# The first weight units of the experts split during the end of the attention, and the first gather's indices written by VectorE

## The chip, the cores and the metric

The kernel runs on one core of a Trainium2 chip, as one launch. A core has TensorE (PE in the profile; its weight loads are PEld), VectorE (DVE), ScalarE (ACT), GpSimd (POOL) and SyncE (SP), which only issues DMAs here. The metric is the device time of one execution in microseconds (us), as the median of several runs. Less is better.

## The reference, cut to what matters

The model is a gated cross-attention layer followed by a mixture of experts in which each expert picks its tokens:

```
x = x + tanh(g_xattn) * attention(layernorm(x), ctx, mask)        # B=8, S=224, D=512, context 750, 16 heads of 32
x = x + tanh(g_ffn)   * ffn(layernorm(x))
ffn(x):                                                            # E=8 experts, I=2048
    affinity = softmax(x @ gate_w.T), turned to (b, e, s)
    gating, idx = top_k(affinity, 56)                              # 56 rows for each batch and expert
    x_in = x[b, idx]                                               # gather
    h = silu(x_in @ w_gate.T) * (x_in @ w_up.T)
    out[b, idx] += gating * (h @ w_down.T)                         # scatter-add
```

All is float32. Expert 0 can start only once the top 56 rows of every batch are known, that is, after the attention and the second layer norm of the last batch.

## The kernel before, in words

There are three stages, each a block of its own. A block ends when every engine has come to its end, and the next one begins then.

**project_context** makes K and V of all batches. **attend** runs over the 8 batches: scores, softmax, values, output projection, residual (`x2`, in the tile `x_res`), second layer norm (`xn2`; the profile calls it `xn`), its rows stored to the DRAM tensor `xn_rows`, the logits of the gate and the affinities. Its functions `end()` (one for each engine) hold what is left for the last batch, and the change is there. On DVE (line 1165) the order is: the two `residual` operations (L1051), `moments` (L964, L967), `norm_2` (L975), the copy of the second half of the turned rows to `xT` (L1177), `logits` (L1061 to L1064), `affinity` (L1069 to L1074), and `rounds`: 7 rounds of MAX8, FIND_INDEX8 and MATCH_REPLACE8 (L1084 to L1086) for the top 56 and then `gate_all` and `row_all` (L1089, L1090). Between `moments` and `norm_2`, POOL turns the variance into 1/sqrt in two small operations (`root`, L780 and L782). POOL then stores the rows (`store_rows`, L810), writes the output rows' base (`x2_out`, two operations of line 795) and stores them (`store_out`, L806). ACT (line 941) copies `c_r` (L893), then the first half of the turned rows (`x2_columns`, L857), then takes the exponential of the logits (L897). PE turns the normed rows (`turn_last`, L1249) and computes the logits (L1262). SP, in its own `end()` (line 752), loads the last residual rows and then, once the last scores are made, the first 4 weight units (L756) into `w_raw`, which lies where `ks` was.

**experts** streams the weights as units of 128 x 1024 float32 (512 KB). There are 24 for each expert: 16 for gate and up, 8 for down. A unit has one of NRAW = 4 slots in each of `w_raw`, `w_hi` and `w_lo`. ACT copies it to fp32r (`ws_hi`, L1502), DVE writes the rest (`ws_lo = w_raw - ws_hi`, L1552), and PE makes three products for each pair of tiles (hi by hi, lo by hi, hi by lo: L1622 to L1624 for gate and up, L1639 to L1641 for down). Both splits run LEAD = 3 units ahead of PE; for the first three units of expert 0 they stand at the very start of this block, on ACT and on DVE. SP loads unit u as soon as the slot's `ws_lo` is written (`wlo_done`); for expert 0 that begins with unit 4.

The block begins with two small products on PE (L1668) that place the gates and the row numbers in `gu_ps[0]`. DVE takes `gate_t` (L1588) and `idx_t` (L1590) from there, POOL copies expert 0's four columns of `idx_t` to `gather_i` (L1469) and issues four indirect DMAs (L1472), each of 112 rows of 2 KB from `xn_rows` to `xg`. When all four have landed, PE turns them (L1608), ACT and DVE split them (`xs_hi` L1507, `xs_lo` L1557), and the first product of expert 0 can run. For the other experts the gather, the turning and the splitting run beside the products of the expert in front. `scatter(e)` copies four indices (L1477) and issues four indirect DMAs that add to the output (L1482).

In this stage the memory holds, from below: `h_hi`, `w_raw`, `w_hi`, `w_lo`, the gates and indices, `xg`, `xs_hi`, `xs_lo`, `silu`, `hid`, `h_lo`, `y_cols`, `y_sb`.

Of the kernel before, what the change touches and what calls it, by code (L numbers as in the profile page):

```python
# [7 lines left out]
F32R = mybir.dt.float32r  # L8
# [6 lines left out]
ds = bass.ds  # L15
# [27 lines left out]
LEAD = 3  # L43
WAYS = 32
# [25 lines left out]
F_XT, F_Q, F_USES = 0, 2, 4  # L70

# [46 lines left out]
def program(nc, ctxT, x, maskq, wk, wv, wq, wo, gatew, gx, gf, wstream, consts, rotations, out):  # L118
# [5 lines left out]
    with ExitStack() as top:  # L124
        def sem(name):
            return top.enter_context(nc.semaphore(name))
# [13 lines left out]
        w_in = [sem(f"w_in{j}") for j in range(NRAW)]  # L140

        with ExitStack() as mid:
# [8 lines left out]
            with ExitStack() as late:  # L151
                sb(late, "below", [P, IC * SLOTS - E_OVER * (KC // 2) * PAIR])
                w_raw = [sb(late, f"w_raw{j}", [P, UNIT]) for j in range(NRAW)]
# [5 lines left out]
                x_t=sb(mid, "x_t", [QP, QC, D]), xn=sb(mid, "xn", [QP, QC, D]), xT=sb(mid, "xT", [P, 2, 2 * S]),  # L159
                q_rot=sb(mid, "q_rot", [P, NG, S]), q_cos=sb(mid, "q_cos", [P, NG, S]),   # L160
                qs=sb(mid, "qs", [3 * WAYS, H, S], F32R), mq=sb(mid, "mq", [QP, QC, SK]),
# [12 lines left out]
                   cos, sin, gains, gate_all, row_all, wstream, w_raw, w_in)  # L174
        experts(nc, sem, sb, ps, w_raw, w_in, wstream, xn_rows, out_rows, cst, ident, gains, gate_all, row_all)
# [429 lines left out]
def attend(nc, sem, sb, ps, both, x, maskq, wo, gatew, kd, vd, xn_rows, out, cst, ident,  # L605
           cos, sin, gains, gate_all, row_all, wstream, w_raw, w_in):

    with ExitStack() as st:
# [77 lines left out]
        with nc.Block() as block:  # L686
            @block.sync
            def _(sp):
# [63 lines left out]
                def end():  # L752
                    load_res(B - 1)
                    hold(m_made, NS * B)
                    for u in range(NRAW):
                        sp.dma_start(w_raw[u][:], wstream[u]).then_inc(w_in[u], 16)  # L756
                    sp.wait_ge(x_in, 16 * (B + 1))
# [95 lines left out]
            def _(act):  # L853
# [87 lines left out]
                def end():  # L941
                    copy_parts(B - 1, NG - 1)
                    x2_columns(B - 1, 0)
                    logit_exp(B - 1)
# [4 lines left out]
            def _(dve):  # L949
# [143 lines left out]

                def start():
                    nc.vector.memset(flags_sb[:], 0.0).then_inc(rest_free, 1)
                    for h in range(MLEAD):
                        for qc in range(QC):
                            mask_scores(0, h, qc)
# [66 lines left out]
                def end():  # L1165
                    b = B - 1
                    normalise(b, NG - 2)
                    affinity(b - 1, (b - 1) % 2)
                    normalise(b, NG - 1)
                    for c in range(QC):  # L1170
                        residual(b, c, m_ps[c][0:QP, 0, :])
                    dve.wait_ge(rest_free, R_USES * b + R_Y + 3)
                    dve.nop(nofuse=True)
                    moments(b, 1, x2)
                    norm_2(b)
                    dve.wait_ge(rest_made, R_USES * b + R_XNT + 2)
                    nc.vector.tensor_copy(xT[:, 1], m_ps[1][:, 1, 0:2 * S]).then_inc(rest_free, 1)  # L1177
                    logits(b)
                    affinity(b, b % 2)
                    rounds()  # L1180
# [217 lines left out]
def experts(nc, sem, sb, ps, w_raw, w_in, wstream, xn_rows, out_rows, cst, ident, gains, gate_all, row_all):  # L1398

    with ExitStack() as st:  # L1400
        h_hi = sb(st, "h_hi", [P, IC, SLOTS], F32R)
        sb(st, "w_raw_place", [P, NRAW, UNIT])
        w_hi = [sb(st, f"ws_hi{j}", [P, UNIT], F32R) for j in range(NRAW)]
        w_lo = [sb(st, f"ws_lo{j}", [P, UNIT], F32R) for j in range(NRAW)]
# [3 lines left out]
        xg = sb(st, "xg", [RP, RG, D])  # L1408
        xs_hi, xs_lo = sb(st, "xs_hi", [P, DC, SLOTS], F32R), sb(st, "xs_lo", [P, DC, SLOTS], F32R)
        silu = [sb(st, f"silu{j}", [P, SLOTS]) for j in range(2)]  # L1410
        hid = [sb(st, f"hid{j}", [P, SLOTS]) for j in range(2)]
        h_lo = sb(st, "h_lo", [P, IC, SLOTS], F32R)
        y_cols = sb(st, "y_cols", [P, DC, SLOTS])
        y_sb = sb(st, "y_sb", [RP, RG, D])
# [5 lines left out]
        whi_done, wlo_done = sem("whi_done"), [sem(f"wlo_done{j}") for j in range(NRAW)]  # L1420
# [16 lines left out]
        with nc.Block() as block:  # L1437
            @block.sync
            def _(sp):
# [10 lines left out]

                for u in range(NRAW, NU):
                    load(0, u)
# [5 lines left out]
            def _(pool):  # L1458
# [5 lines left out]
                def gather(e):  # L1464


                    hold(x_turned, e)
                    hold(gathered, 16 * RG * e)
                    nc.gpsimd.tensor_copy(gather_i[:], idx_t[:, ds(e, 1), :].rearrange("p o g -> p (o g)")).then_inc(gidx_done, 1)  # L1469
                    hold(gidx_done, e + 1)  # L1470
                    for g in range(RG):
                        pool.indirect_dma_start(xg[:, g, :], None, xn_rows, bass.IndirectOffsetOnAxis(gather_i[:, g:g + 1], 0)).then_inc(gathered, 16)  # L1472
# [12 lines left out]
                pool.wait_ge(idx_ready, 1)  # L1485
# [10 lines left out]
            def _(act):  # L1496
# [39 lines left out]

                for u in range(LEAD):
                    split_w(0, u)
# [9 lines left out]
            def _(dve):  # L1548
# [38 lines left out]
                dve.wait_ge(turned, 1)  # L1587
                nc.vector.tensor_scalar(gate_t[:].rearrange("p e g -> p g e"), gu_ps[0][0:RP, 0:RG * E].rearrange("p (g e) -> p g e", g=RG),  # L1588
# [3 lines left out]
                for u in range(LEAD):  # L1592
                    split_w(0, u)
# [144 lines left out]
```

## Time and profile before

| | |
|---|---|
| three runs | 1839.09, 1839.38, 1833.33 us; median 1839.09 |
| the profiled execution | 1836.25 us |
| its span, first to last instruction | 1834.4 us |
| mean granted TensorE clock | 0.981 |
| PE busy | 1740.8 us (95%) |
| DVE, ACT, POOL busy | 1038.9, 839.2, 235.4 us |
| start of the experts' block | 841 us after the span's start |

The rows further down are of the one profiled execution; all their times count from the start of its span. A timeline row gives start, duration, engine, line, operation, written tile, read tiles and shapes, the number of instructions (x3: three, one behind the other, and the duration is then theirs together) and, in brackets, how long the engine had been idle before and what ended that. A row of a stretch gives its bounds and length, then for PE, PEld, DVE, ACT and POOL the busy time with the number of instructions, and then the granted TensorE clock (1.00 is 2.4 GHz, 0.50 is 1.2 GHz), the share of the time that the 16 DMA engines were busy, and GB/s. The chain that ended last is followed back from the last instruction of the kernel, at each step to what released it.

### The profile page before, as it was taken

Reading aid. Unit: us, or ns where it says so; the run is one execution under the profiler, and the core shown is the slowest. Engines: PE = TensorE matmul, PEld = TensorE weight load, DVE = VectorE, ACT = ScalarE, POOL = GpSimd, SP = SyncE. Lnnn points to the kernel's source line nnn. Section 1 sums busy time; section 2 is a strip of 40 time slices with the busy share of each in tenths; the row PEclk is TensorE's granted clock in tenths of the full one; section 3 lists DMA queues with packets and bytes.
Section 4 is the critical chain, followed back from the end, with each engine's and each line's share of the span. In section 5 each row is a group of like instructions: output and inputs, shape, how many; then the busy total and the mean of one; then the engine's idle time right before and its main releaser. Section 6 shows DMA issues by size and latency. Waiting matters only on the chain.

```text
span 1834.4 us, 28481 instructions
## 1 busy us (share of the span) xinstructions
PE 1740.8 (95%) x10502; PEld 1545.1 (84%) x10502; DVE 1038.9 (57%) x1786; ACT 839.2 (46%) x1482; POOL 235.4 (13%) x302
## 2 busy tenths in 40 slices
PE   7999999899999999983999999999999999999995
PEld 6898998677777877753999999999999999999995
DVE  6666667777887787754544535435445354453541
ACT  3223225777776877742433434424344243343430
POOL 0000002131231232122000102002020020010101
PEclk9999999999999999995999999999999999999998
DMA  6544547756755755523333535335343252353421
GB/s 242 224 173 186 189 156 220 182 126 153 178 147 135 183 150 134 141 87 96 115 104 103 150 109 143 103 103 151 106 121 127 106 149 104 101 150 109 124 92 20
DMA packets 76301, 251.90 MB, mean 137 GB/s; under 512 B 10784, under 2 KB 10784, under 8 KB 74928
## 3 DMA queue, kind: packets, MB, share of 16 engines
q1 hardware_dynamic: 64208, 216.55, 38.3%
q0 software_dynamic: 12000, 34.12, 7.9%
q8 instruction: 57, 0.93, 0.2%
q14 instruction: 36, 0.29, 0.1%
HBM read 188.01 MB, written 51.61 MB: 131 GB/s over the span
## 4 chain that ended last, share of the span: by engine, by line
PE 52%; POOL 1%; DVE 0%; issue 0%; DMA 0%; DVEq 0%; ACT 0%; POOLq 0%
PE gu_ps L1624 11%; PE gu_ps L1623 11%; PE gu_ps L1622 11%; PE y_ps L1641 6%; PE y_ps L1640 6%; PE y_ps L1639 6%; PE y_ps L1650 1%; PE gu_ps L1608 1%; POOL out L1482 0%; DMA xg<-xn_rows,gather_i 0%; POOL gather_i L1469 0%; POOL xg L1472 0%; DVE xs_lo L1557 0%; DVE y_cols L1584 0%; PE gu_ps L1668 0%
## 5 line engine op out<-in xcount | busy, mean ns | idle before, releaser
L1622 PE MATMUL gu_ps<-xs_hi,ws_hi 128*128 128x448 f32 x1024 | 370.3, 362 | 3.0 <-DVE xs_lo L1557 3.0
L1624 PE MATMUL gu_ps<-xs_hi,ws_lo 128*128 128x448 f32 x1024 | 371.9, 363 | 0.0
L1623 PE MATMUL gu_ps<-xs_lo,ws_hi 128*128 128x448 f32 x1024 | 371.8, 363 | 0.0
L1552 DVE TENSOR_TENSOR ws_lo<-w_raw,ws_hi 128x1024 fp32r<-128x1024 f32 x192 | 235.2, 1226 | 189.3 <-ACT ws_hi L1502 188.3
L1502 ACT ACTIVATE ws_hi<-w_raw 128x1024 fp32r<-128x1024 f32 x192 | 201.5, 1051 | 163.7 <-PE y_ps L1641 150.6
L1298 PEld LDWEIGHTS t_ps<-cst,sm 112*125 112x125 f32 x1536 | 205.0, 190 | 68.6 <-issue 29.3
L990 DVE CUSTOM_DVE_ANT_0 sm<-m_ps,mq 112x752 f32<-112x752 f32 x256 | 229.7, 935 | 34.2 <-PE m_ps L1282 33.8
L1298 PE MATMUL t_ps<-cst,sm 112*125 112x112 f32 x1536 | 233.3, 281 | 15.0 <-DVE e_t L998 11.3
L880 ACT ACTIVATE sm<-sm,least 112x752 f32<-112x752 f32 x256 | 234.7, 919 | 13.7 <-DVE least L990 12.7
L1622 PEld LDWEIGHTS gu_ps<-xs_hi,ws_hi 128*128 128x128 f32 x1024 | 192.0, 187 | 16.9 <-issue 3.3
L1623 PEld LDWEIGHTS gu_ps<-xs_lo,ws_hi 128*128 128x128 f32 x1024 | 192.7, 188 | 14.6
L1624 PEld LDWEIGHTS gu_ps<-xs_hi,ws_lo 128*128 128x128 f32 x1024 | 192.6, 188 | 10.4
L1523 ACT ACTIVATE silu<-gu_ps 128x448 f32<-128x448 f32 x128 | 69.8, 545 | 274.2 <-PE gu_ps L1624 272.2
L1641 PE MATMUL y_ps<-h_hi,ws_lo 128*128 128x448 f32 x512 | 187.8, 367 | 0.0
L1640 PE MATMUL y_ps<-h_lo,ws_hi 128*128 128x448 f32 x512 | 187.6, 367 | 0.0
L1639 PE MATMUL y_ps<-h_hi,ws_hi 128*128 128x448 f32 x512 | 187.4, 366 | 0.0
L887 ACT ACTIVATE e_t<-t_ps 125x448 f32<-125x448 f32 x256 | 137.4, 543 | 107.6 <-PE t_ps L1298 106.2
L1571 DVE TENSOR_TENSOR hid<-silu,gu_ps 128x448 f32<-128x448 f32 x128 | 79.6, 622 | 188.2 <-ACT silu L1523 188.2
L1482 POOL DMA_INDIRECT out<-y_sb,scatter_i x32 | 52.4, 1637 | 860.5 <-DVE y_sb L1562 853.2
L1574 DVE TENSOR_TENSOR h_lo<-hid,h_hi 128x448 fp32r<-128x448 f32 x128 | 80.0, 625 | 82.5 <-ACT h_hi L1525 81.8
L1282 PE MATMUL m_ps<-ks,qs 96*112 96x376 f32 x512 | 120.0, 355 | 5.0 <-PEq L227 1.7
L1525 ACT ACTIVATE h_hi<-hid 128x448 fp32r<-128x448 f32 x128 | 74.0, 578 | 88.0 <-DVE hid L1571 88.0
(153 smaller groups left out, 2438.6 us busy)
## 6 DMA issues: line engine op xcount, KB each, us to landing
w_raw<-wstream SPq DMA_DIRECT2D x192, 512.0 KB, 3.5
ks<-k_split SPq DMA_DIRECT2D x192, 188.0 KB, 5.4
k_split<-k_split SPq DMA_DIRECT2D x32, 752.0 KB, 3.4
v_rows<-v_out SPq DMA_DIRECT2D x16, 750.0 KB
vs<-v_rows SPq DMA_DIRECT2D x16, 750.0 KB
c_raw<-ctxT SPq DMA_DIRECT2D x7, 1500.0 KB, 13.0
qs<-q_hi POOLq DMA_DIRECT2D x64, 112.0 KB, 5.1
mq_raw<-maskq SPq DMA_DIRECT2D x7, 656.2 KB, 10.9
```

The lines of the kernel that those rows point to most:

```text
L880: nc.scalar.activation(rows, rows, ACT.Exp, bias=least[:, h % KSLOTS, qc:qc + 1], scale=-1.0, accum_out=sums[:, h // HG % 2, qc, h % HG:h ...
L887: nc.scalar.activation(e_t[h % (2 * HG)][:, pc], t_ps[tile_of(b, h, pc) % 2][0:KP, 0:PAIR], ACT.Copy).then_inc(t_act, 1)
L990: nc.vector.tensor_tensor_reduce(sm[:, h % SR, qc].rearrange("p (a n) -> p a n", a=2), m_ps[qc][0:QP, :, 0:KN], mq[:, qc].rearrange("p (a ...
L1298: mm = nc.tensor.transpose(t_ps[n % 2][0:KP, a:a + QP], sm[:, h % SR, qc, c * KP:c * KP + KP], ident[0:QP, 0:QP])
L1502: nc.scalar.activation(w_hi[s][:], w_raw[s][:], ACT.Copy).then_inc(whi_done, 1)
L1552: nc.vector.tensor_tensor(w_lo[s][:], w_raw[s][:], w_hi[s][:], ALU.subtract).then_inc(wlo_done[s], 1)
L1622: nc.tensor.matmul(o, w_hi[s][:, w], xs_hi[:, c], start=(c == 0), stop=False)
L1623: nc.tensor.matmul(o, w_hi[s][:, w], xs_lo[:, c], start=False, stop=False)
L1624: mm = nc.tensor.matmul(o, w_lo[s][:, w], xs_hi[:, c], start=False, stop=(c == DC - 1))
L1639: nc.tensor.matmul(o, w_hi[s][:, w], h_hi[:, i], start=(i == 0), stop=False)
L1640: nc.tensor.matmul(o, w_hi[s][:, w], h_lo[:, i], start=False, stop=False)
L1641: mm = nc.tensor.matmul(o, w_lo[s][:, w], h_hi[:, i], start=False, stop=(i == IC - 1))
```

## The change

It has five parts.

1. `w_raw`, `w_hi`, `w_lo` and their semaphores are made before the attention (`First`). They start 6872 elements up in each partition instead of 7168, and `w_hi` and `w_lo` lie where `ks`, `q_hi`, `q_lo`, `x_t`, `xn`, `q_rot`, `q_cos` and `qs` of the attention were; `xT` is moved out of their way. In the experts, what was above the weights or behind them (`xg`, `y_sb`, `y_cols`, `silu`, gates and indices) lies below them, and `h_hi` lies at the end.
2. The three `ws_hi` copies of units 0 to 2 go from the start of the experts on ACT to ACT's `end()` in the attention, ahead of `x2_columns`.
3. The three `ws_lo` subtractions go to DVE's `end()`: one before `norm_2`, one behind it, one behind the copy to `xT`.
4. The indices of expert 0's gather are written by DVE, straight from `gu_ps[0]`, before `gate_t` and `idx_t`; POOL waits for that alone. Before later gathers POOL waits for `idx_ready` too.
5. SP loads unit 4 and what follows only once the first gather has landed.

```diff
...
+SPARE = 16
+FIRST = 2 * (B // 2) * D + DC * SLOTS + 2 * SLOTS + (2 * E + 2) * (B // 2) + SPARE
...
-        w_in = [sem(f"w_in{j}") for j in range(NRAW)]
...
             with ExitStack() as late:
-                sb(late, "below", [P, IC * SLOTS - E_OVER * (KC // 2) * PAIR])
-                w_raw = [sb(late, f"w_raw{j}", [P, UNIT]) for j in range(NRAW)]
+                sb(late, "below", [P, FIRST - E_OVER * (KC // 2) * PAIR])
+                first = First(
+                    w_raw=[sb(late, f"w_raw{j}", [P, UNIT]) for j in range(NRAW)],
+                    w_hi=[sb(late, f"ws_hi{j}", [P, UNIT], F32R) for j in range(NRAW)],
+                    w_lo=[sb(late, f"ws_lo{j}", [P, UNIT], F32R) for j in range(NRAW)],
+                    w_in=[sem(f"w_in{j}") for j in range(NRAW)], whi_done=sem("whi_done"),
+                    wlo_done=[sem(f"wlo_done{j}") for j in range(NRAW)])
             q_hi, q_lo = sb(mid, "q_hi", [P, NG, S], F32R), sb(mid, "q_lo", [P, NG, S], F32R)
-                x_t=sb(mid, "x_t", [QP, QC, D]), xn=sb(mid, "xn", [QP, QC, D]), xT=sb(mid, "xT", [P, 2, 2 * S]),
-                q_rot=sb(mid, "q_rot", [P, NG, S]), q_cos=sb(mid, "q_cos", [P, NG, S]), 
-                qs=sb(mid, "qs", [3 * WAYS, H, S], F32R), mq=sb(mid, "mq", [QP, QC, SK]),
+                x_t=sb(mid, "x_t", [QP, QC, D]), xn=sb(mid, "xn", [QP, QC, D]),
+                q_rot=sb(mid, "q_rot", [P, NG, S]), q_cos=sb(mid, "q_cos", [P, NG, S]),
+                qs=sb(mid, "qs", [3 * WAYS, H, S], F32R), xT=sb(mid, "xT", [P, 2, 2 * S]), mq=sb(mid, "mq", [QP, QC, SK]),
...
                     hold(m_made, NS * B)
                     for u in range(NRAW):
-                        sp.dma_start(w_raw[u][:], wstream[u]).then_inc(w_in[u], 16)
+                        sp.dma_start(first.w_raw[u][:], wstream[u]).then_inc(first.w_in[u], 16)
...
                 def end():
                     copy_parts(B - 1, NG - 1)
+                    for u in range(LEAD):
+                        act.wait_ge(first.w_in[u], 16)
+                        nc.scalar.activation(first.w_hi[u][:], first.w_raw[u][:], ACT.Copy).then_inc(first.whi_done, 1)
                     x2_columns(B - 1, 0)
                     logit_exp(B - 1)
...
+                def low_w(u):
+                    dve.wait_ge(first.whi_done, u + 1)
+                    nc.vector.tensor_tensor(first.w_lo[u][:], first.w_raw[u][:], first.w_hi[u][:], ALU.subtract).then_inc(first.wlo_done[u], 1)
...
                     dve.wait_ge(rest_free, R_USES * b + R_Y + 3)
                     dve.nop(nofuse=True)
                     moments(b, 1, x2)
+                    low_w(0)
                     norm_2(b)
+                    low_w(1)
                     dve.wait_ge(rest_made, R_USES * b + R_XNT + 2)
                     nc.vector.tensor_copy(xT[:, 1], m_ps[1][:, 1, 0:2 * S]).then_inc(rest_free, 1)
+                    low_w(2)
                     logits(b)
                     affinity(b, b % 2)
                     rounds()
...
     with ExitStack() as st:
-        h_hi = sb(st, "h_hi", [P, IC, SLOTS], F32R)
-        sb(st, "w_raw_place", [P, NRAW, UNIT])
-        w_hi = [sb(st, f"ws_hi{j}", [P, UNIT], F32R) for j in range(NRAW)]
-        w_lo = [sb(st, f"ws_lo{j}", [P, UNIT], F32R) for j in range(NRAW)]
+        xg, y_sb = sb(st, "xg", [RP, RG, D]), sb(st, "y_sb", [RP, RG, D])
+        y_cols = sb(st, "y_cols", [P, DC, SLOTS])
+        silu = [sb(st, f"silu{j}", [P, SLOTS]) for j in range(2)]
         gate_t = sb(st, "gate_t", [RP, E, RG])
         idx_t = sb(st, "idx_t", [RP, E, RG], U32)
         gather_i, scatter_i = sb(st, "gather_i", [RP, RG], U32), sb(st, "scatter_i", [RP, RG], U32)
-        xg = sb(st, "xg", [RP, RG, D])
+        sb(st, "first_place", [P, 3 * NRAW * UNIT + SPARE])
+        w_raw, w_hi, w_lo = first.w_raw, first.w_hi, first.w_lo
         xs_hi, xs_lo = sb(st, "xs_hi", [P, DC, SLOTS], F32R), sb(st, "xs_lo", [P, DC, SLOTS], F32R)
-        silu = [sb(st, f"silu{j}", [P, SLOTS]) for j in range(2)]
         hid = [sb(st, f"hid{j}", [P, SLOTS]) for j in range(2)]
-        h_lo = sb(st, "h_lo", [P, IC, SLOTS], F32R)
-        y_cols = sb(st, "y_cols", [P, DC, SLOTS])
-        y_sb = sb(st, "y_sb", [RP, RG, D])
+        h_hi, h_lo = sb(st, "h_hi", [P, IC, SLOTS], F32R), sb(st, "h_lo", [P, IC, SLOTS], F32R)
-        whi_done, wlo_done = sem("whi_done"), [sem(f"wlo_done{j}") for j in range(NRAW)]
+        w_in, whi_done, wlo_done = first.w_in, first.whi_done, first.wlo_done
...
                         hold(wlo_done[s], raw_uses(e, u))
                     sp.dma_start(w_raw[s][:], wstream[ds(NU * e + u, 1)].rearrange("o p n -> p (o n)")).then_inc(w_in[s], 16)
+                hold(gathered, 16 * RG)
                 for u in range(NRAW, NU):
...
                 def gather(e):
-                    hold(x_turned, e)
-                    hold(gathered, 16 * RG * e)
-                    nc.gpsimd.tensor_copy(gather_i[:], idx_t[:, ds(e, 1), :].rearrange("p o g -> p (o g)")).then_inc(gidx_done, 1)
-                    hold(gidx_done, e + 1)
+                    if isinstance(e, int) and e == 0:
+                        hold(gidx_done, 1)
+                    else:
+                        hold(x_turned, e)
+                        hold(gathered, 16 * RG * e)
+                        hold(idx_ready, 1)
+                        nc.gpsimd.tensor_copy(gather_i[:], idx_t[:, ds(e, 1), :].rearrange("p o g -> p (o g)")).then_inc(gidx_done, 1)
+                        hold(gidx_done, e + 1)
                     for g in range(RG):
                         pool.indirect_dma_start(xg[:, g, :], None, xn_rows, bass.IndirectOffsetOnAxis(gather_i[:, g:g + 1], 0)).then_inc(gathered, 16)
...
                         pool.indirect_dma_start(out_rows, bass.IndirectOffsetOnAxis(scatter_i[:, g:g + 1], 0), y_sb[:, g, :], None,
                                                 compute_op=ALU.add).then_inc(scattered, 16)
-                pool.wait_ge(idx_ready, 1)
                 gather(0)
                 gather(1)
                 scatter(0)
...
-                for u in range(LEAD):
-                    split_w(0, u)
                 split_x(0)
                 act.wait_ge(gates_ready, 1)
                 expert(0, True, False)
...
                 dve.wait_ge(turned, 1)
+                nc.vector.tensor_copy(gather_i[:], gu_ps[0][0:RP, RG * E:2 * RG * E].rearrange("p (g e) -> p g e", g=RG)[:, :, 0:1]
+                                      .rearrange("p g o -> p (g o)")).then_inc(gidx_done, 1)
                 nc.vector.tensor_scalar(gate_t[:].rearrange("p e g -> p g e"), gu_ps[0][0:RP, 0:RG * E].rearrange("p (g e) -> p g e", g=RG),
                                         gains[0:RP, 1:2], None, ALU.mult).then_inc(gates_ready, 1)
                 nc.vector.tensor_copy(idx_t[:].rearrange("p e g -> p g e"),
                                       gu_ps[0][0:RP, RG * E:2 * RG * E].rearrange("p (g e) -> p g e", g=RG)).then_inc(idx_ready, 1)
-                for u in range(LEAD):
-                    split_w(0, u)
                 split_x(0)
                 dve.wait_ge(gates_ready, 1)
                 expert(0, True, False)
...
```

## Rows read from the trace of the kernel before

**Rows 1.** The page: busy time, share of the span and instructions of each engine.

```profile
PE 1740.8 (95%) x10502; PEld 1545.1 (84%) x10502; DVE 1038.9 (57%) x1786; ACT 839.2 (46%) x1482; POOL 235.4 (13%) x302
```

**Rows 2.** The waits of PE, 860 to 1834: us in total, times, longest.

```profile
PE gu_ps L1622 <- DVE xs_lo L1557: 3.0, 1, 3.0
```

**Rows 3.** Stretches: length, busy us (instructions) by engine, granted clock, DMA share, GB/s.

```profile
841.00:854.00 13.00, 0.92 (x4) 0.82 (x4) 3.75 (x5) 2.95 (x3) 7.20 (x5) 0.50 0.59 192
860.47:863.60 3.13, 3.13 (x9) 2.78 (x10) 1.18 (x1) 1.15 (x1) 2.52 (x3) 0.50 0.66 178
982.00:1104.00 122.00, 122.00 (x624) 113.87 (x623) 54.91 (x65) 45.72 (x65) 12.12 (x10) 1.00 0.39 120
```

**Rows 4.** The chain that ended last, 842 to 861: start us, length us, work.

```profile
842.02 0.28 DVE gate_t L1588
842.47 3.36 POOL gather_i L1469
850.55 3.58 DMA xg<-xn_rows,gather_i
854.27 3.23 PE gu_ps L1608 x16
860.47 0.71 PE gu_ps L1622
```

**Rows 5.** Timeline, start of the experts: start, us, instruction [idle before, ended by].

```profile
841.04 2.95 ACT L1502 ACTIVATE ws_hi<-w_raw 128x1024 fp32r<-128x1024 f32 x3 [13.16 <-PEq L686]
842.19 0.21 DVE L1590 CAST idx_t<-gu_ps 112x32 uint32<-112x32 f32 x1
842.28 3.48 DVE L1552 TENSOR_TENSOR ws_lo<-w_raw,ws_hi 128x1024 fp32r<-128x1024 f32 x3
843.58 1.45 SPq L1449 DMA_DIRECT2D w_raw<-wstream  x2
846.71 1.05 POOL L1472 DMA_INDIRECT xg<-xn_rows,gather_i  x1 [0.90 <-POOL gather_i L1469]
857.69 0.18 POOL L1469 COPY gather_i<-idx_t 112x4 uint32<-112x4 uint32 x1 [6.21 <-PE gu_ps L1608]
858.64 0.95 POOL L1472 DMA_INDIRECT xg<-xn_rows,gather_i  x1 [0.77 <-POOL gather_i L1469]
```

**Rows 6.** Timeline of the last scatter, 1816 to 1820.

```profile
1816.12 1.41 DVE L1562 TENSOR_SCALAR y_sb<-y_ps,gate_t 112x512 f32<-112x512 f32 x2 [2.12 <-PE y_ps L1650]
1818.30 1.48 POOL L1482 DMA_INDIRECT out<-y_sb,scatter_i  x1 [85.23 <-DVE y_sb L1562]
```

**Rows 7.** A stretch in which the last gather was being issued.

```profile
851.00:852.00 1.00, 0.00 (x0) 0.00 (x0) 0.00 (x0) 0.00 (x0) 0.48 (x1) 0.50 0.94 277
```

**Rows 8.** DMA issues, 800 to 880: KB each, us from issue to landing.

```profile
out<-x2o POOLq DMA_DIRECT2D x1, 448.0 KB, 3.5
```

**Rows 9.** Timeline, end of the attention, 819 to 828: DVE, POOL and ACT.

```profile
819.04 0.25 DVE L967 BATCH_NORM_AGGREGATE mv<-stats 112x2 f32<-112x6 f32 x2
819.52 0.21 POOL L780 TENSOR_SCALAR var<-mv 112x2 f32<-112x2 f32 x1 [17.61 <-DVE mv L967]
819.89 0.73 POOL L782 TENSOR_TENSOR rstd<-var,minus_half 112x2 f32<-112x2 f32 x1
820.71 1.00 DVE L975 TENSOR_SCALAR xn<-x_res,mv,rstd 112x512 f32<-112x512 f32 x2 [1.42 <-POOL rstd L782]
822.79 0.54 ACT L857 ACTIVATE xT<-w_ps 128x448 f32<-128x448 f32 x1 [12.32 <-PE w_ps L1249]
823.09 3.11 POOL L795 TENSOR_SCALAR x2o<-x_res,flags_sb 112x512 f32<-112x512 f32 x2
823.17 0.62 DVE L1177 COPY xT<-m_ps 128x448 f32<-128x448 f32 x1 [1.46 <-PE m_ps L1249]
827.04 0.17 DVE L1061 COPY lg<-w_ps 112x16 f32<-112x16 f32 x1 [3.25 <-PE w_ps L1262]
```

**Rows 10.** A stretch at the end of the attention's weight loads.

```profile
817.00:818.00 1.00, 0.00 (x0) 0.00 (x0) 0.90 (x2) 0.00 (x0) 0.00 (x0) 1.00 0.23 94
```

More of the change, by code:

```diff
@@ L70 @@
 F_XT, F_Q, F_USES = 0, 2, 4
+@dataclass
+class First:
+    w_raw: object
+    w_hi: object
+    w_lo: object
+    w_in: object
+    whi_done: object
+    wlo_done: object
 @dataclass
@@ L173, in program @@
             attend(nc, sem, sb, ps, both, x, maskq, wo, gatew, kd, vd, xn_rows, out, cst, ident,
-                   cos, sin, gains, gate_all, row_all, wstream, w_raw, w_in)
-        experts(nc, sem, sb, ps, w_raw, w_in, wstream, xn_rows, out_rows, cst, ident, gains, gate_all, row_all)
+                   cos, sin, gains, gate_all, row_all, wstream, first)
+        experts(nc, sem, sb, ps, first, wstream, xn_rows, out_rows, cst, ident, gains, gate_all, row_all)
 def project_context(nc, sem, sb, ps, both, ctxT, wk, wv, wq, x, maskq, gx, gf, consts, rotations, kd, vd, cst, gains):
@@ L605, in attend @@
 def attend(nc, sem, sb, ps, both, x, maskq, wo, gatew, kd, vd, xn_rows, out, cst, ident,
-           cos, sin, gains, gate_all, row_all, wstream, w_raw, w_in):
+           cos, sin, gains, gate_all, row_all, wstream, first):
     with ExitStack() as st:
@@ L1395, in _, with experts @@
                 every_batch(start, body, end)
-def experts(nc, sem, sb, ps, w_raw, w_in, wstream, xn_rows, out_rows, cst, ident, gains, gate_all, row_all):
+def experts(nc, sem, sb, ps, first, wstream, xn_rows, out_rows, cst, ident, gains, gate_all, row_all):
     with ExitStack() as st:
-        h_hi = sb(st, "h_hi", [P, IC, SLOTS], F32R)
-        sb(st, "w_raw_place", [P, NRAW, UNIT])
-        w_hi = [sb(st, f"ws_hi{j}", [P, UNIT], F32R) for j in range(NRAW)]
-        w_lo = [sb(st, f"ws_lo{j}", [P, UNIT], F32R) for j in range(NRAW)]
+        xg, y_sb = sb(st, "xg", [RP, RG, D]), sb(st, "y_sb", [RP, RG, D])
+        y_cols = sb(st, "y_cols", [P, DC, SLOTS])
+        silu = [sb(st, f"silu{j}", [P, SLOTS]) for j in range(2)]
         gate_t = sb(st, "gate_t", [RP, E, RG])
```

## The prediction

> **What bounds the kernel now.** I read the page first: PE is busy for 95% of the span [rows 1], so time can be won only where PE is not working. Then PE's waits from 860 to the end: the first product of expert 0 waits 3.0 us [rows 2], and between 982 and 1104 PE is busy for all 122.00 us at full clock [rows 3]. The seven later experts offer nothing to a change that touches neither the number nor the shape of the matmuls. That leaves the seam between attention and experts: from 841 to 854 PE works 0.92 of 13 us [rows 3]. There I read the chain that ended last. It runs over POOL's copy of the indices (842.47, 3.36 us), four issues of the gather, its landing (3.58 us after the last issue's start, at 854.13), the turning on PE (854.27, 3.23 us), ACT's and DVE's split, and the first product at 860.47 [rows 4]. Ahead of it, in the attention's end, the chain goes through DVE with POOL's square root in between [rows 9]. PE is at half clock throughout this seam, until 3.13 us after the first product [rows 3].
>
> **Part 4, the indices (the gain).** Before, the product that holds the row numbers is followed on DVE by `gate_t` and by `idx_t` (842.19, 0.21 us). POOL's copy starts at 842.47 but lasts until 845.82, although it writes four elements a row; the same copy for expert 1 takes 0.18 us [rows 4, 5]. Its length is that of DVE's three `ws_lo` subtractions (842.28, 3.48 us, to 845.76): it ends 0.06 us after them [rows 5]. So about 3.2 us of the copy is waiting for DVE. Then 0.90 us pass and the first gather is issued at 846.71 [rows 5].
>
> After, DVE writes the indices as its first operation. DVE's first operation there, `gate_t`, starts at 842.02, and `idx_t` follows at 842.19 for 0.21 us [rows 4, 5]; I take 0.2 us for the copy, hence 842.2. How long POOL then needs to its first issue is seen where it waits for DVE ahead of an indirect DMA: `y_sb` ends at 1816.12 + 1.41 = 1817.53 and the scatter is issued at 1818.30, 0.77 us later [rows 6]. So the first gather is issued at 842.97, **3.74 us earlier**. Bounds: POOL's copy started 0.07 us after `idx_t` ended (842.40 to 842.47), and the longest gap was 0.90 [rows 5], so 3.6 to 4.4. The first issue took 1.05 us, and 0.95 for expert 1 [rows 5]: 0.1 more.
>
> **Part 5, the held loads (a second, smaller gain).** Before, three weight loads of 512 KB were issued from 843.58 on, as the slots' `ws_lo` ended [rows 5], 3 us ahead of the gathers. The DMA engines were still 0.94 busy between 851 and 852, when the last gather was being issued [rows 7]. After, the four gathers have the engines to themselves. How fast would the last one land? A store of 448 KB issued by POOL on otherwise idle engines lands 3.5 us after its issue [rows 8]; a gather has half the bytes, 0.8 us less at the 277 GB/s of [rows 7], so 2.7 us against 3.58 [rows 4]: **0.9 us**. Bounds: 0 (the row scatter of a gather is slower than a plain store) and 1.5.
>
> The cost: units 4 to 6 are loaded only from about 849 on. At the 277 GB/s of the crowded stretch [rows 7] their 1.5 MB take 5.7 us, so the third is in by about 856. ACT needs unit 4 only after PE has finished unit 0, about 6 us after the first product, and units 5 and 6 later still. The cover is over 5 us; without it each us late would be a us on PE.
>
> **Parts 2 and 3, the splits moved into the attention (the cost).** At the start of the experts, the three copies on ACT (841.04, 2.95 us) and the three subtractions lay beside a wait for the gather that lasted until 854 [rows 5, 4]: taking them away gives nothing beyond what stands under part 4. Moved, they cost what follows.
>
> On ACT, the copies wait for the units, and `x2_columns` is behind them. The DMA engines finish the units in 817 to 818 (share 0.23) [rows 10]. Even if all three copies ran after 818 they would end at 821, and ACT is idle for 12.32 us before 822.79 [rows 9]: nothing, with 1.8 us to spare. If that cover goes, PE's logits wait for ACT.
>
> On DVE, `low_w(0)` is put between `moments` (ends 819.29) and `norm_2` (820.71) [rows 9]. It takes 1.23 us or less (3.48 / 3 = 1.16 each in a row [rows 5]), and the gap is 1.42 us: by DVE alone it fits. But in that gap POOL works: the variance at 819.52 for 0.21 us, then the power at 819.89 for 0.73 [rows 9]. Both read SBUF beside a subtraction with two inputs in SBUF, as the copy of the indices did when it stood still for 3.2 us [rows 5]. DVE has `low_w(0)` next in its order and starts it at about 819.25, ahead of POOL. So POOL's first operation ends at about 820.5 instead of 819.73, and `norm_2` starts at 821.5: **0.8 us later**. Bounds: 0 if POOL gets in first, and 1.3 if the wait repeats at the power.
>
> `low_w(1)` runs from 822.5 to 823.7, while PE turns the rows; the copy to `xT` was ready at 823.17 and now is at 823.97 [rows 9]: hidden, with 0.2 us to spare. `low_w(2)` starts at about 824.6, and the logits come at 827.04 + 0.8 = 827.84: hidden unless it starts later than 826.6. POOL's `x2_out` reads SBUF too (3.11 us for two [rows 9]); it will be held by up to 1.2 us for `low_w(2)`. Nobody waits for it before the block ends at 841: the output store, issued about 2 us later than now, lands before 833.
>
> By the rows, `low_w(2)` simply holds POOL. The Trainium skill (SBUF — State Buffer, the section on the shared port pair) says that the pair is locked for a whole instruction and that the one that starts first gets it. By that rule DVE would be the one held, since `x2_out` is running when `low_w(2)` comes up. The trace of before shows no DVE operation held by POOL. If DVE gets in between the two operations of `x2_out`, the sum is unchanged; if it has to let both pass, the logits come 0.4 us later and the sum is -3.5. Rival C has the same place, with POOL's own durations.
>
> **Part 1, the places in memory.** No instruction, no byte and no wait is added by it, apart from a wait for `idx_ready` that has long been met in POOL's later gathers. No row shows a duration that depends on an address. I take 0.
>
> **The clock.** The first 9 matmuls after 860.47 ran at half clock, 3.13 us [rows 3], which costs 1.6 us against full clock. Coming 4 us earlier, this stretch may be shorter or longer. I take 0, with 1.6 to either side.
>
> **The sum.** -3.74 - 0.1 - 0.9 + 0.8 = -3.9 us: first product at 856.6 instead of 860.47, and everything after it moved by as much. The profiled execution took 1836.25 us for a span of 1834.4: 1832.3 after. Against the median of 1839.09 it would be 1835.2. The profiled execution is 2.8 us below the median and within the three runs, which spread over 6 us; I give a figure between the two, **1834.0**.
>
> **The rivals.**
> - A: `low_w(0)` costs nothing. For it: DVE's gap of 1.42 us is longer than 1.23, and POOL's operands are only two elements a row. Against it: four elements a row did not save the index copy. -4.7 us, 1833.2.
> - B: the gather lands no sooner without the loads, because its own issues and short rows set its pace. For it: four issues 1.25 us apart carry only 224 KB each, 180 GB/s, under the 277 GB/s seen [rows 7]. Against it: the engines were nearly full. -3.0 us, 1834.9. With 0 instead of 0.8 us at the square root it is back at the forecast.
> - C, slower than before: DVE and POOL stand in each other's way at the end of the attention, so that the subtractions come into line. `low_w(2)` waits for both operations of `x2_out`, 3.11 us, and the three subtractions' 3.48 us are all exposed: up to 6.6 us against a gain of 4.7, so +1.9 us, 1839.8. It decides from 4.7 us on. For it: the held index copy, and the small margin of 0.2 us at `xT`. Against it: waiting for `x2_out` alone moves `low_w(2)` from 824.6 to 827.0, its end to 828.2, and the logits by only 0.4 us; two of the subtractions have PE's work beside them.
> - D: the new places change the pace of the experts (either sign). Half a per cent would need 1.2 us for each of the eight experts. Against it: nothing but PE's own issue sets the pace there [rows 3], and that doesn't change.
>
> **How the numbers follow.** Forecast 0.50, A 0.17, B 0.18, C 0.06, D and the rest 0.09, half of it on each side. About 0.5%, 9.2 us, is what a measurement of this kernel can tell from no change. Forecast, A, B and C all lie within it: same 0.90. Faster, under 1829.9: 0.06, from D and from a median that falls as low as the lowest run of before (1833.33 - 3.9 = 1829.4). Slower: 0.04. The range: from 1829.4 to 1839.8, which holds the bounds of every term on either base and C; I round it to 1829.5 to 1839.5.
>
> **What would show it.** Right: no `ws_hi` or `ws_lo` at the start of the experts; a copy to `gather_i` of about 0.2 us on DVE; the first gather issued 1.9 us after the block's start and not 5.7; weight loads behind the gather's landing; 3.8 us less between the block's start and the landing by POOL's part, and 0.9 more by the DMAs'; POOL's variance ended by DVE and `norm_2` 0.8 us later. Wrong: `norm_2` where it was (A); the last gather still over 3.4 us to land (B); DVE idle before `low_w(2)` and the logits late by over 1 us (C); an expert that takes longer or shorter than 122 us (D).

## The result, and the profile after

The changed kernel takes 1853.66 us (median of 6 runs, 1851.32 to 1857.11) against 1837.53 us for the kernel before (6 runs, 1833.33 to 1839.63). The ratio is 1.0091, 95% interval 1.0073 to 1.0108: **slower by 0.9%**, where 1834.0 was forecast and 0.5% was put as what can be told from no change. The profiled execution took 1854.84 us, its span is 1853.0 us.

The seam, from the end of the attention to the first product of the experts, gets shorter, though by less than forecast. In the chain that ended last (start us, length us, work) the index copy on DVE takes 0.17 us, and the first gather is issued 2.03 us after the block's first product, not 5.65 [rows 4, 5]:

```profile
842.61 0.94 PE gu_ps L1694 x4
843.57 0.17 DVE gather_i L1614
843.79 0.85 issue
844.64 1.04 POOL xg L1501
...
848.47 3.46 DMA xg<-xn_rows,gather_i
...
852.06 3.24 PE gu_ps L1634 x16
...
858.26 0.44 PE gu_ps L1648
```

The end of the attention, from the timeline of the changed kernel, answers to [rows 9]. POOL's variance takes 0.95 us instead of 0.21 and ends after DVE's subtraction; `norm_2` (`xn`) starts 2.76 us after the aggregate instead of 1.67:

```profile
819.51 0.25 DVE L986 BATCH_NORM_AGGREGATE mv<-stats 112x2 f32<-112x6 f32 x2
819.67 1.19 DVE L1116 TENSOR_TENSOR ws_lo<-w_raw,ws_hi 128x1024 fp32r<-128x1024 f32 x1
819.99 0.95 POOL L796 TENSOR_SCALAR var<-mv 112x2 f32<-112x2 f32 x1 [17.61 <-DVE mv L986]
821.09 0.73 POOL L798 TENSOR_TENSOR rstd<-var,minus_half 112x2 f32<-112x2 f32 x1
822.27 1.00 DVE L994 TENSOR_SCALAR xn<-x_res,mv,rstd 112x512 f32<-112x512 f32 x2 [1.41 <-POOL rstd L798]
...
824.65 3.27 POOL L811 TENSOR_SCALAR x2o<-x_res,flags_sb 112x512 f32<-112x512 f32 x2
824.73 0.62 DVE L1203 COPY xT<-m_ps 128x448 f32<-128x448 f32 x1 [0.32 <-PE m_ps L1276]
...
825.27 1.22 DVE L1116 TENSOR_TENSOR ws_lo<-w_raw,ws_hi 128x1024 fp32r<-128x1024 f32 x1
...
828.60 0.17 DVE L1080 COPY lg<-w_ps 112x16 f32<-112x16 f32 x1 [2.12 <-PE w_ps L1289]
```

From the start of the last batch's `residual` operations to the first product of expert 0 it was 815.94 to 860.47, 44.53 us; it is 816.40 to 858.26, 41.86 us. So the seam won 2.7 us. The loss is behind it. From the first to the last product of the experts it was 860.47 to 1812.35, and is 858.26 to 1831.13: 951.9 us against 972.9, **21.0 us more for the same 4608 products**. PE waits for nothing there. In the stretch of [rows 3] (PE's columns come first) it is busy for all 122.00 us at full clock, as before, but it starts 610 matmuls where it started 624:

```profile
982.00:1104.00 122.00, 122.00 (x610) 111.39 (x609) 54.06 (x64) 45.37 (x65) 11.64 (x10) 1.00 0.40 119
```

The timeline of PE shows it product by product. A gate-and-up stage has 384. In expert 1 the first starts at 980.42 and the last at 1061.31: 80.89 us, and 78.37 before. A start comes 0.20 or 0.21 us after the one in front of it in every unit alike, whatever ACT, DVE and the DMAs do meanwhile; only where the next expert's rows are turned is there one longer gap (1.87 us), and that was so before. First come two lines of the kernel before, the first and the last product of this stage, then the lines of the changed kernel:

```profile
979.47 0.37 PE L1622 MATMUL gu_ps<-xs_hi,ws_hi 128*128 128x448 f32 x1
1057.84 0.36 PE L1624 MATMUL gu_ps<-xs_hi,ws_lo 128*128 128x448 f32 x1
```

```profile
980.42 0.37 PE L1648 MATMUL gu_ps<-xs_hi,ws_hi 128*128 128x448 f32 x1
980.63 0.37 PE L1649 MATMUL gu_ps<-xs_lo,ws_hi 128*128 128x448 f32 x1
...
1061.10 0.37 PE L1649 MATMUL gu_ps<-xs_lo,ws_hi 128*128 128x448 f32 x1
1061.31 0.37 PE L1650 MATMUL gu_ps<-xs_hi,ws_lo 128*128 128x448 f32 x1
```

The gate-and-up stages went from 78.37 us to 80.89 and 80.06 in turn (17.7 us over eight experts), the down stages from 40.45 to 40.70 and 40.91 (3.3 us).

### The profile page after: what moved, and what is told of

Read it like the earlier page. It is cut to its first block, busy times and chain, and to the rows that moved or that the text cites. A ratio compares the mean times of both kernels' runs of the same rounds, so it can differ in the third digit from the quotient of the medians.

```text
span 1853.0 us, 28489 instructions
## 1 busy us (share of the span) xinstructions
PE 1764.0 (95%) x10502; PEld 1546.8 (83%) x10502; DVE 1039.4 (56%) x1787; ACT 840.5 (45%) x1482; POOL 230.4 (12%) x301
## 4 chain that ended last, share of the span: by engine, by line
PE 53%; POOL 0%; DVE 0%; issue 0%; DMA 0%; DVEq 0%; ACT 0%; POOLq 0%
PE gu_ps L1650 11%; PE gu_ps L1648 11%; PE gu_ps L1649 11%; PE y_ps L1667 6%; PE y_ps L1665 6%; PE y_ps L1666 6%; PE y_ps L1676 1%; PE gu_ps L1634 1%; POOL out L1511 0%; DMA xg<-xn_rows,gather_i 0%; POOL xg L1501 0%; DVE xs_lo L1583 0%; DVE y_cols L1610 0%; PE gu_ps L1694 0%; DVE y_sb L1588 0%
## 5 line engine op out<-in xcount | busy, mean ns | idle before, releaser
L1648 PE MATMUL gu_ps<-xs_hi,ws_hi 128*128 128x448 f32 x1024 | 378.3, 369 | 3.0 <-DVE xs_lo L1583 3.0
L1650 PE MATMUL gu_ps<-xs_hi,ws_lo 128*128 128x448 f32 x1024 | 377.9, 369 | 0.0
L1649 PE MATMUL gu_ps<-xs_lo,ws_hi 128*128 128x448 f32 x1024 | 376.2, 367 | 0.0
```

Of the source, the lines that this page charges most:

```text
L1648: nc.tensor.matmul(o, w_hi[s][:, w], xs_hi[:, c], start=(c == 0), stop=False)
L1649: nc.tensor.matmul(o, w_hi[s][:, w], xs_lo[:, c], start=False, stop=False)
L1650: mm = nc.tensor.matmul(o, w_lo[s][:, w], xs_hi[:, c], start=False, stop=(c == DC - 1))
```

## The experiments

A product on PE has two operands in memory: the weights (`ws_hi`, `ws_lo`), which are loaded first, and the moving rows that then pass through them (`xs_hi` and `xs_lo` for gate and up, `h_hi` and `h_lo` for down). Below, an address is the byte in a partition at which a tile starts. In the kernel before, `w_raw` starts at 48576, `ws_hi` at 64960, `xs_hi` at 106240, `h_hi` at 19904 and `h_lo` at 127744. In the changed kernel these are 47392, 63776, 96576, 114496 and 143168. The slots of the weights follow each other at 4096 bytes, tiles of 448 columns at 1792 = 7 x 256. A stage's length is always start of first to start of last product, in experts 1 to 6.

**e1, e2, e3, e4: the places or the schedule?** Four kernels separate part 1 from parts 2 to 5.

```diff
# e1: the changed kernel, weights 32 bytes up
-                sb(late, "below", [P, FIRST - E_OVER * (KC // 2) * PAIR])
+                sb(late, "below", [P, FIRST + 8 - E_OVER * (KC // 2) * PAIR])
# e2: the kernel before, weights 32 bytes up
-                sb(late, "below", [P, IC * SLOTS - E_OVER * (KC // 2) * PAIR])
+                sb(late, "below", [P, IC * SLOTS + 8 - E_OVER * (KC // 2) * PAIR])
...
-        sb(st, "w_raw_place", [P, NRAW, UNIT])
+        sb(st, "w_raw_place", [P, NRAW * UNIT + 8])
...
+        sb(st, "pad", [P, 8])
         gate_t = sb(st, "gate_t", [RP, E, RG])
# e3: the changed kernel with FIRST = IC * SLOTS and the experts' tiles in the order of before
# e4: the changed kernel with its hunks of attend's end(), gather, load(0, u) and split_w(0, u) undone
```

> The changed kernel with w_raw, w_hi and w_lo 32 bytes higher in each partition (from byte 47424 on instead of 47392, a multiple of 64 now), nothing else moved. Theory 1, the first byte of the weights decides the pace of PE: the gate-and-up stage of an expert goes back from 80.9 / 80.1 us to 78.4, and with the seam 2 to 3 us shorter than before the time is about 1835, 0.998 to 1.000 of the kernel before. Theory 2, the order of the tiles (h_hi above the weights, xg and y_sb below them) decides: about 1854, 1.009. Theory 3, the new schedule of the seam sets a phase that lasts: 1854, 1.009.

> The kernel before with w_raw, w_hi and w_lo 32 bytes higher (from byte 48608 on instead of 48576, no longer a multiple of 64); all tiles above them moved by 64 bytes. Theory 1: the gate-and-up stages take 80 to 81 us instead of 78.4, the whole about 1856 (1.010). Theories 2 and 3: 1837, ratio 1.000, stages of 78.4.

> Parts 2 to 5 of the change with all tiles of the experts where they were in the kernel before (weights from byte 48576 on). Theories 1 and 2: stages of 78.4 us and the time of the kernel before less the gain of the seam, 1834 to 1836, ratio 0.998 to 0.999. Theory 3, the schedule: 1854, 1.009.

> Part 1 of the change alone: the new places, with splits, indices and loads as in the kernel before. Theories 1 and 2: stages of 80 to 81 us and about 1856 to 1857 (1.010 to 1.011), slower than the changed kernel by the 2.2 us of the seam. Theory 3: 1837, ratio 1.000.

Measured, as ratios to the kernel before: e1 1.0022 (1.0011 to 1.0034), e2 1.0086 (1.0069 to 1.0103), e3 0.9987 (0.9977 to 0.9996), e4 1.0079 (1.0062 to 1.0096). The stretch 982 to 1104 of e3, and then of e4:

```profile
982.00:1104.00 122.00, 122.00 (x624) 113.86 (x623) 55.93 (x66) 46.92 (x66) 12.12 (x10) 1.00 0.40 119
```

```profile
982.00:1104.00 122.00, 122.00 (x610) 111.45 (x609) 54.07 (x64) 45.42 (x64) 11.64 (x10) 1.00 0.40 119
```

So the places alone carry the loss, with the same alternation of 80.89 and 80.06 us: from the first to the last product of the experts e4 takes 972.5 us, 20.6 more than before, and e3 only 0.8 more. The schedule alone is a small gain, from 1838.58 to 1836.16 us, and the whole gain of the seam is its: 41.87 us in e3, 44.54 in e4. The forecast for e4, 1.010 to 1.011 and slower than the changed kernel, was missed: with four runs spread over 7 us, the times don't show the 2.7 us of the seam that the traces show. Thirty-two bytes are enough: e2 has nothing of the change, and its stages take 80.39 us. Theory 2, the order of the tiles, and theory 3, the schedule, fall. But e1 came back only to 79.36 us, not to 78.4, so "a multiple of 64" alone was not the rule.

**e5 to e8: weights against moving rows.** All are the changed kernel with other paddings. `below` moves the weights, `first_place` the moving rows (`xs`, `h`). In the last line the first figure stands in place of `FIRST` and the second in place of `SPARE` (16), in elements of 4 bytes:

```diff
-                sb(late, "below", [P, FIRST - E_OVER * (KC // 2) * PAIR])
-        sb(st, "first_place", [P, 3 * NRAW * UNIT + SPARE])
# e5: FIRST - 8, + 0    e6: FIRST + 8, + 32    e7: FIRST - 8, + 8    e8: FIRST - 8, + 16
```

> The changed kernel with the first byte of every tile that PE reads in the experts (w_hi, w_lo, xs_hi, xs_lo, h_hi, h_lo) a multiple of 128. Measured so far for an expert's gate-and-up stage: 78.4 us with weights at 64 past a multiple of 128 and xs at 0; 79.4 with both at 64; 80.1 to 80.9 with weights at 32 and xs at 64. Theory 1a, each tile counts by itself and 0 is best: 78.4 or less, 40.2 or less for the down stage, the whole at or under 0.9985. Theory 1b, what counts is the distance between weights and moving rows, and being equal is bad: 79.4, about 1.002. Theory 1c, only multiples of 64 count and the 1 us between 78.4 and 79.4 has another cause (order of the tiles): 79.4, 1.002, as the two layouts below too.

> The changed kernel with the weights at 64 past a multiple of 128 and xs and h at a multiple of 128, as weights and xs were in the kernel before, but in the new order. Theories 1a and 1b: stage of 78.4 us, about 0.998. Theory 1c, the order: 79.4, 1.002.

> The changed kernel with the weights at a multiple of 128 and xs and h at 32 past one. If the odd 32 bytes cost through the weight loads alone: 78.4 to 79.4 us a stage, about 1.000. If through either read of PE: 80 to 81, about 1.009.

> The changed kernel with the weights at a multiple of 128 and xs and h at 64 past one. Theory 1a: between 78.4 and 79.4 us a stage, the moving rows' 64 costing what it costs; theory 1b (equal is bad, unequal good): 78.4, 0.998; theory 1c: 79.4, 1.002.

e5 1.0025 (1.0014 to 1.0036), e6 0.9946 (0.9929 to 0.9963), e7 1.0095 (1.0075 to 1.0115), e8 0.9953 (0.9933 to 0.9973). The gate-and-up stages took 79.37, 78.36, 80.78 and 78.36 us. Theory 1a fails on e5, 1c on e6 and e8; 1b fits these three, and e7 only adds that 32 apart is slower than equal: what counts is the distance. The ratios of e6 and e8 were forecast at 0.998 and came out lower, mostly because the down stages fell too, from 40.45 to 39.76 us, 5.6 us over eight experts. The stretch of e6:

```profile
982.00:1104.00 122.00, 122.00 (x627) 114.45 (x626) 55.41 (x67) 47.44 (x67) 12.12 (x10) 1.00 0.41 123
```

**e9: the rule tried on the kernel before, and missed.**

```diff
-                sb(late, "below", [P, IC * SLOTS - E_OVER * (KC // 2) * PAIR])
+                sb(late, "below", [P, IC * SLOTS + 32 - E_OVER * (KC // 2) * PAIR])
...
+        sb(st, "pad0", [P, 16])
         h_hi = sb(st, "h_hi", [P, IC, SLOTS], F32R)
-        sb(st, "w_raw_place", [P, NRAW, UNIT])
+        sb(st, "pad1", [P, 16])
+        sb(st, "w_raw_place", [P, NRAW * UNIT])
```

> The kernel before with h_hi 64 bytes higher, at a multiple of 128, and everything above it by 128 bytes, which leaves its place against 128 as it was: weights at 64, xs and h_lo at 0, now h_hi at 0 too. Nothing of the change is in it. If the pace of PE is set by the distance between the weights and the moving rows (64 apart is fast, equal is slow, 32 is slowest): gate-and-up stages stay at 78.4 us, down stages fall from 40.45 to 39.75, 8 x 0.7 = 5.6 us, 1832 to 1833, ratio 0.997. If the gain of the new order came from the order itself: ratio 1.000.

Ratio 0.9998 (0.9988 to 1.0007). The down stages took 40.18 us, not 39.75. Mod 128 all distances were 64 there; mod 256 `h_lo` lay 64 above the weights and `h_hi` 192. That led to the next four.

**e13 to e16: mod 128, mod 256, or multiples of 64?** e13 is `FIRST + 8, + 64`, e14 `FIRST + 8, + 48`, e16 `FIRST, + 24`; e15 is e9 with `pad1` of 48 and `below` 64 elements up instead of 32.

> The changed kernel with weights at 64 and xs and h at 0 past a multiple of 256 (moving rows 192 above the weights, taken mod 256; in all fast stages so far they were 64 above). If distances are told apart mod 128: stages of 78.4 and 39.8 us, 1830, 0.995. If mod 256 and only 64 above is fast: 79 to 80 and 40.2 us or more, 1840 or over.

> The changed kernel with weights at 64 and xs and h at 192 past a multiple of 256 (128 apart). If distances count mod 128 this is as when equal: 79.4 and 40.3 us, 1842, 1.002. If mod 256 with only equal slow: 78.4 and 39.8, 1830.

> The kernel before with h_hi 64 bytes higher and all tiles above it 256 bytes higher: weights at 192, xs, h_hi and h_lo all at 0 past a multiple of 256, so every moving row is 64 above the weights. Nothing else of the change. Mod 256: the down stage falls from 40.45 to 39.76 us, 8 x 0.7 = 5.6 us, ratio 0.997. If it was the order of the tiles that made the down stages fast in the new layout: 40.2 as in the run with h_hi moved by 64 alone, ratio 0.999 to 1.000.

> The changed kernel with its weights where they are (32 past a multiple of 64) and xs and h moved up by 32, so that they are 64 above the weights but no start is a multiple of 64. If the distance alone counts: 78.4 and 39.8 us, 1830, 0.995. If each start has to be a multiple of 64 too: 80 to 81 us, 1853 to 1858.

e13 1.0008 (0.9997 to 1.0019), e14 1.0107 (1.0089 to 1.0126), e15 0.9973 (0.9959 to 0.9986), e16 0.9956 (0.9944 to 0.9969). e13 came out as forecast for mod 256. In e14 both forecasts were missed: 128 apart is neither as slow as equal (79.4 us) nor fast, but slower than both. The stretches of e14, e15 and e16, in this order:

```profile
982.00:1104.00 122.00, 122.00 (x616) 112.50 (x615) 54.18 (x65) 46.06 (x65) 11.49 (x10) 1.00 0.40 121
```

```profile
982.00:1104.00 122.00, 122.00 (x628) 114.45 (x627) 55.31 (x66) 46.02 (x65) 12.11 (x10) 1.00 0.41 120
```

```profile
982.00:1104.00 122.00, 122.00 (x627) 114.47 (x626) 55.63 (x66) 46.57 (x66) 12.12 (x10) 1.00 0.40 119
```

Put together, with the distance from the weights up to the moving rows, mod 256, for the stages whose moving tiles all lie at one distance:

| distance | gate-and-up stage, us | down stage, us | kernels |
|---|---|---|---|
| 64 | 78.36 | 39.76 | e6, e8, e15, e16 (before, e3 and e9: the gate-and-up stage only) |
| 0 | 79.36 | 40.25 | e1, e5 |
| 192 | 79.20 | 40.18 | e13 |
| 96 | 80.39 | | e2 |
| 32 | 80.78 | 40.70 | e7; the changed kernel and e4: 80.06 and 80.89, 40.70 and 40.91 |
| 128 | 80.78 | 40.63 | e14 (79.88 and 40.50 in expert 1) |

That the distance decides and not the places themselves is shown for 64, with the weights at 0, 32, 64 or 192 past a multiple of 256, and for 0, with them at 0 or 64; 192, 96 and 128 were tried in one layout each. The two layouts with 32 differ a little in how their two paces mix. e16 settles that the multiple of 64 plays no part: all its tiles start 32 bytes off one, and it is as fast as any. e15 settles it for the kernel before: the forecast from the rule was 0.997, measured 0.9973.

The table doesn't add up where a stage has moving tiles at two distances. In the down stage of the kernel before (`h_hi` at 0, `h_lo` at 64) the 23 gaps inside a unit of 24 products take 4.68 or 4.69 us, more than 4.66 with both at 0 (e1) and 4.60 with both at 64. So more than each product's own distance counts, and no run here says what.

**e10 to e12: the seam, in the fast layout of e6.**

```diff
# e10
-                    low_w(0)
                     norm_2(b)
-                    low_w(1)
+                    low_w(0)
...
-                    low_w(2)
+                    low_w(1)
+                    low_w(2)
                     logits(b)
# e11
-                hold(gathered, 16 * RG)
# e12: the splits of units 0 to 2 again at the start of the experts, on ACT and DVE
```

> The layout with weights at 64 and moving rows at 0 (1829.9 measured), with the first low part behind norm_2 and the other two behind the copy to xT, so that no subtraction of DVE lies beside POOL's square root. Theory: norm_2 starts 1.67 us after the last aggregate as in the kernel before, instead of 2.76, and the logits are not later: 1.1 us less up to the first product, about 1828.8. Rival: the two subtractions in a row hold the logits or POOL's x2_out, and nothing is won.

> The layout with weights at 64 and moving rows at 0, without part 5: the loads of units 4 to 6 are issued at once at the start of the experts, beside the first gather. Theory that the loads slow the gather: the last gather lands more than 0.5 us later than the 3.4 us after issue that it takes with part 5. Rival: landing is set by the gather itself, 3.4 to 3.6 us, the same first product.

> The layout with weights at 64 and moving rows at 0, with parts 2 and 3 undone: the three copies and subtractions again at the start of the experts, the indices still written first by DVE (part 4). Theory: the indices are what counted, so the first gather is issued 2.0 to 2.5 us after the block's first product as in the changed kernel, and the 1.1 us of norm_2 come back: the first product of expert 0 comes 1.1 us earlier than with the splits in the attention. Rival: POOL's issues are held by the subtractions as its copy was, and the first issue is at 5 us or later.

From the start of the last batch's `residual` operations to the first product: e6 41.67 us, e10 40.60, e11 41.81, e12 43.27. The ratios (e10 0.9944, e11 0.9958, e12 0.9959, each with some 0.0015 to either side) can't tell these apart, the traces can. In e10 POOL is free again and `norm_2` comes 1.67 us after the aggregate; the two subtractions in a row only hold `x2_out` (4.32 us), which nobody waits for. The logits come 8.00 us after the aggregate, as in the kernel before, and not 9.09 as in the changed one:

```profile
821.51 0.25 DVE L986 BATCH_NORM_AGGREGATE mv<-stats 112x2 f32<-112x6 f32 x2
821.99 0.21 POOL L796 TENSOR_SCALAR var<-mv 112x2 f32<-112x2 f32 x1 [17.61 <-DVE mv L986]
...
823.18 1.00 DVE L994 TENSOR_SCALAR xn<-x_res,mv,rstd 112x512 f32<-112x512 f32 x2 [1.43 <-POOL rstd L798]
...
825.56 4.32 POOL L811 TENSOR_SCALAR x2o<-x_res,flags_sb 112x512 f32<-112x512 f32 x2
...
829.51 0.17 DVE L1080 COPY lg<-w_ps 112x16 f32<-112x16 f32 x1 [0.98 <-PE w_ps L1289]
```

In e11 the last gather lands 3.42 us after the start of its issue, with the loads beside it, and in e6 3.27 us without them; the first product comes 0.14 us later. That is all that can be given to part 5, and the same landing took 3.46 us in the changed kernel, also without the loads. In e12 the rival has the mechanism right, though not the time at which it put the first issue. The first issue begins 2.02 us after the block's first product, as the theory said, and not at 5 us or later. But it lasts 3.66 us instead of 1.04, to 0.9 us past the end of DVE's three subtractions, and the first product comes 1.6 us later than in e6 instead of 1.1 us earlier:

```profile
844.33 0.16 DVE L1610 CAST gather_i<-gu_ps 112x4 uint32<-112x4 f32 x1 [1.27 <-PE gu_ps L1692]
...
844.66 3.48 DVE L1574 TENSOR_TENSOR ws_lo<-w_raw,ws_hi 128x1024 fp32r<-128x1024 f32 x3
845.39 3.66 POOL L1495 DMA_INDIRECT xg<-xn_rows,gather_i  x1 [15.58 <-DVE gather_i L1610]
849.36 0.94 POOL L1495 DMA_INDIRECT xg<-xn_rows,gather_i  x1 [0.30 <-issue]
```

e10 beats both kernels: 1829.3 us, 0.9944 (0.9930 to 0.9958) of the kernel before.

## Why the prediction was wrong

- **The failing step is part 1, "I take 0", and the argument against rival D**: "nothing but PE's own issue sets the pace there, and that doesn't change". PE was indeed busy for all 122.00 us, but being busy is not a pace. Where its two operands start against each other sets how far apart the matmuls start: the 23 gaps inside a gate-and-up unit take 4.60 us in the fast layouts, 200 ns each, and 4.70 or 4.75 us in the changed kernel, 204 or 207 ns. The distance went from 64 to 32 for `xs`, and from 0 and 64 to 32 for `h_hi` and `h_lo`. The loss was 21.0 us; the places alone (e4) cost 20.6, the schedule alone (e3) 0.8. D had the right place, with a chance of under 9% for both signs together; the half per cent that it spoke of is 1.2 us an expert, and it was 2.6.
- The places of the kernel before gave a hint that I left unread: the 23 gaps inside a down unit took 4.68 or 4.69 us, against 4.60 in a gate-and-up unit. It is the same instruction with the same shapes. There `h_hi` lay 0 and `h_lo` 64 above the weights.
- Part 4 was right in mechanism and nearly in size: the first issue comes 3.62 us earlier where 3.74 was forecast (0.90 us from the end of DVE's copy to it, and not 0.77). The further 0.1 us for a shorter first issue didn't come: 1.04 us against 1.05.
- Part 4's gain needs the moved subtractions of part 3, which the sum counts only by their cost. With them back at the start of the experts (e12), they hold POOL's issue as they held its copy: the seam is 43.27 us, against 41.67 in e6 and 44.53 before. The splits moved without part 4 were not run.
- Part 5 is rival B: 0.12 us, not 0.9. Between 849 and 850, while the last gather is on its way, the DMA engines are now 0.69 busy, where they were 0.94 busy during the last gather before [rows 7], and in the last microsecond 0.21. It still takes 3.46 us. What sets that length is not shown.

```profile
849.00:850.00 1.00, 0.00 (x0) 0.00 (x0) 0.00 (x0) 0.00 (x0) 0.40 (x1) 0.50 0.69 199
851.00:852.00 1.00, 0.00 (x0) 0.00 (x0) 0.00 (x0) 0.00 (x0) 0.00 (x0) 0.50 0.21 82
```

- `low_w(0)`: 1.09 us, not 0.8. POOL's variance came 0.74 us later as worked out. The rest, 0.36 us between the end of `rstd` and `norm_2` (0.45 against 0.09 before), is gone in e10; why it is there stays open.
- The seam's sum was -3.9 and came out at -2.7: B is 0.8 us of the difference, the larger cost of `low_w(0)` 0.3 and part 4 with its first issue 0.2. Rival C did not happen: `low_w(2)` took 1.22 us, and the logits are late by no more than `norm_2` is.

The rule of the Trainium skill (SBUF — State Buffer, Who interferes with whom) that the one who starts first keeps the other out is not what this trace shows for DVE: `low_w(2)` started at 825.27 while `x2_out` was running and was not held at all; POOL lost 0.16 us over its two operations (3.27 against 3.11), where the prediction had allowed for up to 1.2. The Trainium skill infers in the same section that descriptor generation needs the pair's write side alone, so that a subtraction with two SBUF inputs should not hold it; in e12 an indirect issue, which reads its indices, was held 2.6 us past its usual length.

## What to carry to other kernels

When tiles that TensorE reads are moved, compare the distance of moving rows and weights mod 256 before and after (this is measured for one type and shape only), and look at the number of matmuls in a fixed stretch and not at busy time. Where stages of the same instruction differ in pace, padding a tile may be worth more than a rearranged wait: 16 and 48 elements of padding gave the kernel before 0.27% (e15), the whole new schedule 0.13% (e3). A DVE subtraction with both inputs in SBUF should not stand beside a POOL operation on the path: moving one away brought 1.07 us (e10 against e6).

## What was not expected of the hardware

- fp32r matmuls of 448 columns at full clock start 200 to 207 ns apart (the gaps inside a unit), by where their moving rows start against their weights. 64 bytes above the weights, mod 256, is the best of the six distances measured; 32 and 128 are the worst. Distances that are no multiple of 32 and other shapes weren't tried, and the mechanism behind it is not known from these runs. Two distances in turn can be slower than either alone (4.69 us for the 23 gaps in the down stage of the kernel before).
- At a distance of 32 there are two paces, 4.70 and 4.75 us for the 23 gaps in a unit. PE passes from one to the other only where turned rows interrupt the products, at every second such place in the changed kernel from expert 1 on, so that its stages alternate, and at each in e7, where every stage has both. The same alternation in e4 shows that it does not hang on the schedule.
